# Turning the rounded attention weights by DMA from SBUF to SBUF, and ones in the pads of the values

## The reference, cut to what matters

```
L0: x += A1(ln(x), ln(x))   quantised self-attention, 16 heads of 16
    x += A2(ln(x), context) quantised cross-attention, 16 heads
    x += geglu(ln(x))
L1: x += SA(rms(x)); x += CA(rms(x), context); x += swiglu(rms(x))    16 heads
L2: x += MH(ln(x), ln(context)), 8 heads of 32; then a recurrence over the 256 tokens
L3: a cross-attention in which the softmax runs over the queries
```

```python
def _fq(x, delta, zp, n_bits):
    xq = jnp.clip(round(x / delta) + zp, 0.0, 2.0 ** n_bits - 1.0)
    return (xq - zp) * delta
attn = jax.nn.softmax(sim, axis=-1)
out = jnp.einsum('bhij,bhjd->bhid', _fq(attn, dw, 0.0, 8), _fq(v, dv, 128.0, 8))
```

## Time and profile before

| | |
|---|---|
| median of 3 runs | 3233.84 us (3232.46 to 3250.25) |
| the profiled execution | 3241.35 us, of which the span is 3239.5 us |
| PE | 2702.2 us busy (83%), granted clock 0.863 of full speed |
| DVE | 1863.5 us (58%) |
| ACT | 1481.2 us (46%) |
| POOL | 684.0 us (21%) |
| stages | first to about 2690 us, recurrence to about 2895 us, third to 3239.5 us |

### The profile page before, as it was taken

One profiled execution on the slowest core, in us unless ns is written; L12 is line 12 of the kernel. 1 busy time (PEld: TensorE's weight loads), 2 busy tenths in 40 slices (PEclk: granted clock), 3 DMA queues, 4 the chain that ended last, 5 costly groups with the idle time before them and its releaser, 6 DMA issues. The chain is left out here.

```text
span 3239.5 us, 52743 instructions
## 1 busy us (share of the span) xinstructions
PE 2702.2 (83%) x19640; PEld 1954.3 (60%) x19640; DVE 1863.5 (58%) x4255; ACT 1481.2 (46%) x3426; POOL 684.0 (21%) x872
## 2 busy tenths in 40 slices
PE   4789888989898899898989889889888774447997
PEld 3567666766666667676767667667666552334443
DVE  4964668575666566756675757576654420004676
ACT  3754356454454544444554535464443211224564
POOL 2410122121211111211211211122111000004775
PEclk9799899989897979797989899999897865558999
DMA  4000000000000000000000000000000001001110
GB/s 174 2 2 1 10 9 3 9 2 9 2 9 2 9 2 9 2 9 2 9 2 9 2 9 2 10 1 8 1 5 1 5 0 39 0 0 32 31 36 24
DMA packets 19675, 40.46 MB, mean 12 GB/s; under 512 B 2528, under 2 KB 10032, under 8 KB 18672
## 3 DMA queue, kind: packets, MB, share of 16 engines
q1 hardware_dynamic: 12976, 17.32, 1.9%
q10 hardware_dynamic: 6464, 19.93, 1.6%
HBM read 27.80 MB, written 9.44 MB: 11 GB/s over the span
## 5 line engine op out<-in xcount | busy, mean ns | idle before, releaser
L955 PE MATMUL psum<-hT,w_l 128*128 128x256 f32 x2048 | 488.9, 396 | 13.5 <-ACT hT L1277 8.7
L955 PEld LDWEIGHTS psum<-hT,w_l 128*128 128x128 f32 x2048 | 400.3, 199 | 87.7 <-issue 16.8
L682 POOL TENSOR_TENSOR rstd<-ms,half 128x2 f32<-128x2 f32 (+1 forms) x144 | 100.2, 696 | 1198.2 <-DVE ms L1042 810.3
L1375 ACT ACTIVATE work<-psum 128x1024 f32<-128x1024 f32 (+1 forms) x224 | 221.0, 1022 | 278.8 <-PE psum L880 227.8
L1359 ACT ACTIVATE work<-psum,nbias,qs 128x256 f32<-128x256 f32 x512 | 282.6, 573 | 46.5 <-DVE nbias L1145 44.8
L1391 ACT ACTIVATE work<-psum,offset 128x1024 bf16<-128x1024 uint16 (+1 forms) x192 | 210.2, 1117 | 188.2 <-PE psum L892 157.6
L773 PE MATMUL psum<-hT,w_l 128*128 128x256 f32 x896 | 241.7, 422 | 15.2 <-ACT hT L1277 12.9
L1277 ACT ACTIVATE hT<-psum,cols 128x256 f32<-128x256 f32 x256 | 122.2, 532 | 244.7 <-PE psum L764 244.2
L722 POOL TENSOR_SCALAR work<-work 128x1024 f32<-128x1024 f32 x128 | 135.1, 1055 | 459.4 <-DVE work L1212 446.4
L967 PE MATMUL psum<-w_l,work 128*128 128x256 f32 x1024 | 227.9, 381 | 1.6 <-DVE work L1235 1.0
L1189 DVE RECIPROCAL work<-psum 128x256 f32<-128x256 f32 x96 | 168.3, 1753 | 94.9 <-PE psum L932 94.8
(11 more groups left out here) (178 smaller groups left out, 4995.9 us busy)
## 6 DMA issues: line engine op xcount, KB each, us to landing
w_l<-in_w_l ACTq DMA_DIRECT2D x1, 5120.0 KB, 24.4
x_res<-in_x SPq DMA_DIRECT2D x16, 256.0 KB, 2.7
res<-x_res ACTq DMA_DIRECT2D x16, 256.0 KB, 2.3
w_l<-res SPq DMA_DIRECT2D x16, 256.0 KB, 2.8
out<-w_l ACTq DMA_DIRECT2D x16, 256.0 KB, 2.0
w_l<-in_w_l ACTq DMA_DIRECT2D x1, 3072.0 KB, 12.7
w_l<-in_w_l SPq DMA_DIRECT2D x2, 1024.0 KB, 8.6
w_l<-in_w_l ACTq DMA_DIRECT2D x2, 1024.0 KB, 16.1
```

What stands on the lines that cost most here:

```text
L955: mm = eng.matmul(banks.tile(key)[:, h * TOKENS:(h + 1) * TOKENS], w1[:, k, h, m * P:(m + 1) * P], hT[p][:, k, :], start=(k == 0), stop=(k ...
L1375: eng.activation(pt(n, p)[0:a.kp, :], banks.pair(key)[0:a.kp, :, :].rearrange("p r n -> p (r n)"), ACT.Exp) \
```

## The change

`turn` moves from PE to the SP queue: one DMA with transpose a part, from a new bf16 buffer `rounded_part` (two a stream) to the place where `evacuate` wrote; `evacuate` goes. The rounding writes bf16 to `rounded_part`: one POOL instruction for A1 as before, two DVE instructions for A2 instead of one. A2's parts are turned in 8 blocks of 128 columns, of which 77 count. The ring of exponentials has 2 buffers (`HELD`) instead of 3, and the rounding of part n waits for the turn of part n - 2. The loads become tasks of SP's planned order, between the turns. In SA and CA the other 16 columns of a head's values hold ones, so that a product gives values and sums; half the products of `soft_weigh` go. `outputs` is rewritten with 32x32 block transposes of DVE around a reciprocal of 8 columns. A1's values need zeros beside them in the same buffer, which POOL sets once a sample (`zeros`) after CA of p - 3.

```diff
-OFFSET = 16384
-MAGIC16 = MAGIC + OFFSET
-RING = 3
+RING, HELD = 3, 2
+TURN, LAND = 2.5, 2.5
@@ quantised (plan)
-                s = work.add("tensor", "scores", ..., q, k, turned.get(2 * u + i - RING), ...
+                s = work.add("tensor", "scores", ..., q, k, rounds.get(2 * u + i - HELD), ...
-                e = work.add("pool" if a.self_attn else "vector", "round", ..., 2.05 if a.self_attn else 0.45, e)
-                turned[2 * u + i] = work.add("tensor", "turn", a, (u, i), p, 0.85, e, ...
-                evacuated.append(work.add("scalar", "evacuate", a, (u, i), p, 1.1, turned[2 * u + i], ...
+                e = work.add("pool" if a.self_attn else "vector", "round", ..., 2.05 if a.self_attn else 1.0, e,
+                             turned.get(2 * u + i - HELD))
+                rounds[2 * u + i] = e
+                turned[2 * u + i] = work.add("sync", "turn", a, (u, i), p, TURN, e,
+                                             weighed if a.self_attn else None, v if a.self_attn else None)
+                evacuated.append(turned[2 * u + i])
@@ sync
+                def turn(a, part, p):
+                    u, i = part
+                    ft, tile = a.units[u]
+                    if a is A1 and ft:
+                        eng.wait_ge(*banks.at(("o", a.name, 0, p)))
+                    elif a is A1:
+                        eng.wait_ge(*v_ready_v.at((a.name, p)))
+                    else:
+                        eng.wait_ge(*banks.at(("o", A1.name, KT - 1, p)))
+                    eng.wait_ge(*(probs_ready_p if a is A1 else probs_ready_v).at((a.name, u, i, p)))
+                    if a is A1:
+                        dst = ptb(p)[:, 8 * i:8 * i + 8, tile * P:(tile + 1) * P]
+                    else:
+                        dst = ptb2(p)[:, 16 * ft + 8 * i:16 * ft + 8 * i + 8, :]
+                    eng.dma_start(dst, rounded_part(a, u, i, p), transpose=True).then_inc(...)
+                steps = {"load": load, "turn": turn}
+                for kind, a, n, p in ORDER["sync"]:
+                    steps[kind](a, n, p)
@@ pool
+                def zeros(a, n, p):
+                    if p < STREAMS:
+                        return
+                    eng.wait_ge(*banks.at(("o", CA.name, KT - 1, p - STREAMS)))
+                    for j in range(2):
+                        eng.memset(vpadb(p)[:, :, j::2, 16 + 16 * j:32 + 16 * j], 0.0).then_inc(...)
                 def round_off(a, part, p):
+                    if 2 * u + i >= HELD:
+                        eng.wait_ge(*turned[part_slot(u, i, p)].at((a.name, *before(u, i), p)))
                     eng.wait_ge(*norm_step.at(("up", a.name, u, i, p)))
-                    eng.tensor_scalar(e, e, 1.0, MAGIC16, ALU.mult, ALU.add)...
+                    eng.tensor_scalar(rounded_part(a, u, i, p), e_part(a, u, i, p), MAGIC, -MAGIC, ALU.add, ALU.add)...
@@ tensor
                 def weigh(a, ft, p):
-                    ready(key, (pt_ready_a, (a.name, 2 * ft + 1 if a is A1 else ft, 1, p)), ...)
+                    for u in ((2 * ft, 2 * ft + 1) if a is A1 else (ft,)):
+                        for i in range(2):
+                            eng.wait_ge(*turned[part_slot(u, i, p)].at((a.name, u, i, p)))
@@ soft_weigh
-                    heads = 2 if a.heads == 16 else 1
-                    for col, ones in ((0, False), (TOKENS, True)):
-                        for j in range(heads):
-                            for c in range(4):
+                    for j in range(2):
+                        for c in range(4):
+                            if a is MH:
+                                v = onesp[0:CTX, :] if j else vc[:, p % STREAMS, (4 * ft + c) * 32:(4 * ft + c + 1) * 32]
+                            else:
+                                v = vpad[p][0:a.kp, kt, ft * 8 + 2 * c + j, :]
@@ vector
                 def outputs(a, ft, p):
-                    eng.reciprocal(rc(p)[:, ft, :], banks.tile(key)[:, TOKENS:2 * TOKENS])...
-                    eng.tensor_tensor(oT[p][:, ft, :], banks.tile(key)[:, 0:TOKENS], rc(p)[:, ft, :], ALU.mult) ...
+                    if a is MH:
+                        eng.transpose(turned, banks.tile(key)[:, TOKENS:2 * TOKENS])...
+                        eng.reciprocal(few, turned.rearrange("p (b c) -> p b c", c=32)[:, :, 0])...
+                        eng.transpose(rc(p)[:, ft, :], bcast(few.unsqueeze(2), [P, 8, 32]))...
+                        eng.tensor_tensor(oT[p][:, ft, :], banks.tile(key)[:, 0:TOKENS], rc(p)[:, ft, :], ALU.mult) ...
+                        return
+                    eng.transpose(wide, banks.tile(key))...
+                    for j in range(2):
+                        ins = eng.reciprocal(few[:, j, :], by_head[:, j, :, 16 * (1 - j)])
+                    for j in range(2):
+                        ins = eng.tensor_tensor(narrow..., by_head[:, j, :, 16 * j:16 * j + 16], bcast(few[:, j, :]...), ALU.mult)
+                    eng.transpose(oT[p][:, ft, :], narrow)...
                 def round_off(a, part, p):
-                    eng.tensor_scalar(e, e, 255.0, MAGIC16, ALU.min, ALU.add)...
+                    eng.tensor_scalar(e, e, 255.0, MAGIC, ALU.min, ALU.add)...
+                    if 2 * u + i >= HELD:
+                        eng.wait_ge(*turned[part_slot(u, i, p)].at((a.name, *before(u, i), p)))
+                    eng.tensor_scalar(rounded_part(a, u, i, p)..., e..., -MAGIC, None, ALU.add) ...
@@ scalar
-                def evacuate(a, part, p):
-                    ...
-                    eng.activation(dst, banks.tile(key).bitcast(U16)..., ACT.Identity, bias=offset[0:a.kp, :]) ...
```

More of the change, by code:

```diff
@@ L104, in order @@
                     todo.append(b)
[L105 removed]
+        end, free = {}, {"tensor": 0.0, "vector": 0.0, "scalar": 0.0, "pool": 0.0, "sync": 0.0, "clock": 0.0}
         order, holder = {e: [] for e in free}, [None] * 8
@@ L279, in context_of @@
             before = [earlier(p, "tensor", "context_" + what, MH, 0) for what in ("keys", "values")]
+            before = [work.add("clock", "loaded", "ctx", 0, p, LAND, work.add("sync", "load", "ctx", 0, p, 0.3, *before))]
             before.append(("scalar", "store", None, 0, p - STREAMS - 1) if p > STREAMS else None)
@@ L298, in plan @@
         late.append(("scalar", "store", None, 0, p - STREAMS - 1) if p > STREAMS else None)
-        x = work.add("clock", "load", None, 0, p, 5.5, earlier(p, "scalar", "store", None, 0))
+        x = work.add("clock", "stored", None, 0, p, LAND, earlier(p, "scalar", "store", None, 0)) if p >= STREAMS else None
+        x = work.add("sync", "load", "x", 0, p, 0.3, x)
+        x = work.add("clock", "loaded", "x", 0, p, LAND, x)
         x = quantised(A1, p, *norm("ln1", p, *late, x))
@@ L306, in plan @@
         used = [("tensor", "context_" + what, CA, 0, p) for what in ("keys", "values")]
-        c = work.add("vector", "moments", "lnc", 0, p, 0.5, earlier(p, "tensor", "norm", "lnc", 0), *late)
+        c = work.add("sync", "load", "tok", 0, p, 0.3, earlier(p, "tensor", "norm", "lnc", 0))
+        c = work.add("clock", "loaded", "tok", 0, p, LAND, c)
+        c = work.add("vector", "moments", "lnc", 0, p, 0.5, c, *late)
         c = work.add("pool", "rstd", "lnc", 0, p, 0.7, c)
@@ L577, in build @@
         r_stored = [sig(f"r_stored{p}", 16) for p in range(STREAMS)]
+        turned = [sig(f"turned{n}", 16) for n in range(STREAMS * HELD)]
         u_stored = [sig(f"u_stored{p}", 16) for p in range(STREAMS)]
@@ L633, in _, with load @@
                 ctx_all = t["ctx"]
[L634 to L638, removed]
[L640 to L647 removed]
+                def load(what, n, b):
+                    if what == "tok":
+                        if b >= STREAMS:
+                            eng.wait_ge(*banks.at(("lnc", b - STREAMS)))
+                        eng.dma_start(ctok[b][:, :], ctx_all[b]).then_inc(*tok_loaded[b % STREAMS].next(b))
+                    elif what == "ctx":
+                        if b >= STREAMS:
+                            eng.wait_ge(*banks.at(("v", "mh", b - STREAMS)))
+                        eng.dma_start(ctxT[:, b % STREAMS, :, :].rearrange("p b c -> p (b c)"), ctxT_all[b]) \
+                            .then_inc(*c_loaded[b % STREAMS].next(b))
+                    else:
+                        if b >= STREAMS:
+                            eng.wait_ge(*r_stored[b % STREAMS].at(b - STREAMS))
+                        eng.dma_start(x_res[b][:, :, :], x_all[b]).then_inc(*x_loaded[b % STREAMS].next(b))
@@ L882, in scores_t @@
                     mm.then_inc(*banks.filled(key))
-                def turn(a, part, p):
-                    u, i = part
-                    key = ("t", a.name, u, i, p)
-                    ready(key, (probs_ready_p if a is A1 else probs_ready_v, (a.name, u, i, p)))
-                    low = e_part(a, u, i, p).bitcast(BF16).rearrange("p (n b) -> p n b", b=2)[:, :, 0]
-                    for n in range(8):
```

(6 more changed lines are left out.)

160 lines of the change are left out of this document (86 added, 74 removed).

## The result

The changed kernel takes 3120.84 us (median of four, 3116.02 to 3128.91), before 3233.9 beside it: ratio 0.9651, 95% interval 0.9622 to 0.9679. That is 113 us less; the forecast was 189 less, 3045 us, with a range of 2955 to 3215.

What follows compares the result with a forecast made beforehand. PE, 89% busy in the first stage's steady part, was taken as the bound. Savings of 233 us less 45 for new waits plus 3 in the tail gave 191, so 3045 us (5.8% less), range 2955 to 3215.

Steps and rivals of the forecast that it cites:

- the signs: First stage: end near 2500 us, PE busy 210 to 250 us less, landings 3 to 5 us, `weigh` waits under 60.
- The lower bound of 2955: Whole kernel: fast end of the forecast range in us, for savings of 299; chance of a time below it 0.06.
- the largest savings: PE in the first stage: upper bound of its savings, 299 us, where 233 were forecast and 171 was the lower bound.
- Ones: PE, SA and CA: 96 parts lose 16 product instructions each, 96 us saved, between 83 and 116.
- Turns: PE: 192 turns of 8 transposes go, 114 us, plus 23 us of idle time before them.
- it takes 1.05: POOL's rounding in A1: planned at 2.05 us, taken as 1.05, so it gives back 1.0 us of a turn's lateness.
- A bound engine with less work doesn't get emptier, it finishes sooner: PE in the first stage: the argument against its clock falling and giving the gain back.
- The first rival: PE's steady work: clock falls to 0.85, costing 120 us, kernel at 3165 us; chance 0.10, shared with lesser waits.
- The new wait: PE before `weigh`: a turn by DMA takes 4.3 us, so 64 products wait 0.7 us each, 45 us lost.
- second and third rival: Turns by DMA: late at 9 us, kernel 3300 us, chance 0.10; DMA queue the bound at 14.4 us, some 3500, 0.07.
- SP's queue: SP's strict order: waiting turns hold loads behind them; nothing counted, 30 us if 13 loads each delayed a turn 2.3 us.
- DVE: DVE's work: reciprocals and products go, transposes and a second A2 rounding come, net 6 us less, hidden by PE.

Runs made afterwards that it cites:

- e2: Against the kernel before: only the ones in the pads and the new outputs, turns still on PE, old rounding and ring of 3; 3132.8 us, ratio 0.9689.
- e1: Against the changed kernel: POOL's A1 rounding as two instructions instead of one with two additions, same order; 3088.0 us, ratio 0.9555.
- e6: Against e1: a third buffer for A1's rounded parts, so rounding of part n waits for the turn of n - 3; 3090.4 us, ratio 0.954.
- e4: Against the changed kernel: planner told 3.9 us for A1's rounding, 1.1 for A2's, 3.4 for a turn, only the order changes; 3221.3 us, ratio 0.9965.
- e7: Against e1: planner told 2.4 us for the rounding and 3.4 for a turn, same instructions in another order; 3175.1 us, ratio 0.9802.

## Why the prediction was right, and where it was off

**Direction and bound: right.** PE's instructions set the pace where the three streams are at different steps: middle, 114.7 us off for 124 us less PE work. Of the signs, the landings (3.1 us), the waits of `weigh` (53.9) and the clock of the middle (0.88) came out as said; the stage ended at 2574 us and not near 2500, PE lost too little busy time (below), and POOL waited 51.4 us for turns where little was expected. The lower bound of 2955 isn't what the largest savings give, 3234 - 299 = 2935; nothing hangs on it here.

**Ones: right.** 96 forecast, 103 measured alone in e2, in an order of its own.

**Turns: 92 forecast (137 less 45), 13 to 15 measured alone; with the ones in place and a fast rounding 45 (e2 to e1), between kernels of different orders.** This is where the 76 us went, as far as such kernels can tell. Three steps of the prediction failed in it.

- "it takes 1.05": the price of the old instruction was given to a new one with other operations. It takes 3.64, the rounding gives nothing back, it is 1.6 us late instead. 33 us of the kernel by e1.
- The sum was made over 16 samples from a row that begins at 220 us. The gain holds per sample in the middle (forecast for the change (233 - 45) / 16 = 11.8, measured 14.3) and outside it not at all: eight samples gave 115 us, the other eight nothing in sum. What was overlooked is that with three streams in A1 DVE is the busiest engine, and that POOL's rounding and DVE's small instructions get in each other's way. That this caused the opening's loss is read from the timeline and not shown; e1, where DVE is held as much in each part (1.11 us instead of 0.23, below), still gained 20 us there. So the shares of POOL's length, DVE's holds, the 22.1 us of waits for turns and the smaller ring of exponentials stay open.
- The clock. "A bound engine with less work doesn't get emptier, it finishes sooner" is true of the middle (0.89 to 0.88), and false of the opening, where PE's clock went from 0.90 to 0.85. Its 862 busy us at 0.90 would be an estimated 862 x 0.85 / 0.90 = 814: some 45 us of PE's time came back that way, part of it where DVE hid it. The first rival was in part what happened; over the stage PE's busy time fell by 177 us and not by the 210 to 250 of the prediction's check.

**The new wait: right in size, by luck.** 45 us forecast for `weigh`, 53.9 measured. A turn lands 3.1 us after the start of its issue where 4.3 were counted, and the rounding before it takes 2.6 more. 64 waits of 0.7 us were counted; there were 22 of 2.5 us at the mean, as before only 30 of the 64 `weigh` waited. POOL did wait for turns, 51.4 us in ten waits, and e6, without them, is no faster than e1. That landings over 7 us would decide (second and third rival) wasn't put to the test: the longest was 4.8.

**SP's queue: no cost of the loads was seen, but turns do stand in it.** Most of SP's new waits are for roundings. Two others stand before a turn (L687) whose rounding may long be done: for the first product of its sample, which still reads the place where the turn will write, and for the values. SP of the changed kernel:

```profile
SPq L682 <- POOL work L775: 772.1, 104, 58.6
SPq L682 <- DVE work L1296: 561.2, 50, 36.4
SPq L687 <- PE psum L954: 259.9, 9, 31.2
...
SPq L687 <- DVE vpad L1122: 104.3, 11, 14.8
```

With the plan's order laid beside the trace, 42 of A1's 128 turns are issued 5 to 32 us after their rounding, and none of A2's over 1 us. The prediction had no such wait. In e4 only six of A1's are over 1 us late, and e4 is 100 us slower, so this lateness doesn't decide the time by itself.

**DVE: -6 forecast, +36 measured**, without new work of that size: `outputs` and the rounding came within 0.3 us a piece of their prices. Old instructions got longer, by 39 us in the sum of their durations; in e1 by 24, in e2, with the old rounding, not at all. The multiplication by the reciprocals of the sums and the small step before it, in the changed kernel; before, they took 353 ns and 357:

```profile
L1285 DVE TENSOR_SCALAR work<-work,rsum 128x256 f32<-128x256 f32 x512 | 164.7, 384 | 4.5
...
L1278 DVE TENSOR_SCALAR rsum<-rden,qs 128x4 f32<-128x4 f32 x128 | 56.7, 443 | 4.7
```

In e2 they are at 353 and 359 ns, as before.

## What to carry to other kernels

Price an instruction by a row with the same operations, not by one of the same engine, shape and place: here the pair of operations alone made it 1.05 or 3.64 us. Multiply a gain by the iterations in which that engine is the bound, and look at the opening, where all streams stand at the same step, by itself. Before reading a change of one or two per cent in a kernel whose order is planned, move a planner's number a little and see how far the time goes: here 22 to 71 us by one number and 87 by three, and the two plans with the measured costs (e4, e7) were the slowest of their instructions.

## What the runs showed of the hardware

- A POOL `tensor_scalar` of 128x1024 f32 takes 1.05 us for (multiply, add) to f32 and for (add, multiply) to bf16, each with a factor of 1.0, and 3.64 for (add, add) and (add, subtract) to bf16.
- A DMA with transpose, 128x1024 bf16 from SBUF to SBUF, lands 3.1 us after the start of its issue and holds the issuing SP for the first 1.23 of them.
- DVE waits for POOL. In e1, POOL and then DVE:

```profile
84.12 1.04 POOL L779 TENSOR_SCALAR work<-work 128x1024 bf16<-128x1024 f32 x1
```
```profile
84.08 1.11 DVE L1198 TENSOR_SCALAR nbias<-nmax,qs 128x4 f32<-128x4 f32 x1
```

The DVE instruction, 0.23 us alone, ends with POOL's, at 85.2. The Trainium skill ("SBUF — State Buffer", Who interferes with whom) says that a DVE `tensor_scalar` can run in a mode that shares ports with POOL, and that then whoever issues first has them for the whole instruction while the other is blocked. Whether this one runs in that mode no row shows. The length of the hold agrees; by the records DVE began first, by 0.04 us, and yet was the one held. With the slow rounding it isn't so. POOL of the changed kernel, beside DVE's 0.91 us from 87.34:

```profile
87.19 3.62 POOL L775 TENSOR_SCALAR work<-work 128x1024 bf16<-128x1024 f32 x1
```

DVE is free again at 88.25, 1.06 us after POOL's start, and runs on beside the rest of POOL's 3.62 us.
